# Graph attention on one core: the aggregation of the four heads in halves of 256 columns

## The reference

```python
h = (x @ W).reshape(N, H, C)
al_s = jnp.einsum('nhc,hc->nh', h, a_src)
al_d = jnp.einsum('nhc,hc->nh', h, a_dst)
e = jax.nn.leaky_relu(al_s[src] + al_d[dst], NEG_SLOPE)
m = jax.ops.segment_max(e, dst, num_segments=N)
ex = jnp.exp(e - m[dst])
denom = jax.ops.segment_sum(ex, dst, num_segments=N)
alpha = ex / (denom[dst] + 1e-16)
msg = h[src] * alpha[:, :, None]
out = jax.ops.segment_sum(msg, dst, num_segments=N)
...
h = jax.nn.elu(_gat_layer(x, src, dst, W1, att_src1, att_dst1, b1, concat=True))
out = _gat_layer(h, src, dst, W2, att_src2, att_dst2, b2, concat=False)
...
x = _layernorm(x + out)
```

## Time and profile before

| | |
|---|---|
| Time, median of 3 runs | 1033.69 us (1031.19 to 1034.45) |
| The profiled execution | 1031.99 us, of which its span (first to last instruction) is 1030.2 us |
| PE busy | 913.7 us, 89% of the span, 4740 instructions |
| Weight loads | 786.4 us, 76% |
| DVE / ACT / POOL busy | 619.3 / 401.3 / 210.1 us |
| The four heads (aggregation and `make`) | from 220 to 676 us of the span |

### The profile page before, as it was taken

How to read it: one execution, slowest core, us unless ns; L and a number is a source line. 1 busy time by engine, 2 the same in 40 slices (tenths; PEclk the granted TensorE clock), 3 DMA queues, 4 the chain that set the end, 5 groups by cost and what they waited for, 6 DMA issues and landing times.

```text
span 1030.2 us, 13905 instructions
## 1 busy us (share of the span) xinstructions
PE 913.7 (89%) x4740; PEld 786.4 (76%) x4740; DVE 619.3 (60%) x1305; ACT 401.3 (39%) x574; POOL 210.1 (20%) x113
## 2 busy tenths in 40 slices
PE   0676788979999999999999999979999998479996
PEld 0454566668787788878887788869999998479995
DVE  9666568379987456863578645443221222988874
ACT  6454531256651366514663155542111112622220
POOL 1002000225530145202442023410000000343432
PEclk9987999989999999999999999989999999689998
DMA  6009975040115410263003431252111100101122
GB/s 155 1 7 191 150 227 171 7 128 27 32 32 191 179 31 29 66 219 126 30 30 102 138 103 37 93 191 111 58 63 40 74 6 1 44 21 57 59 64 69
DMA packets 38710, 86.65 MB, mean 84 GB/s; under 512 B 17251, under 2 KB 17411, under 8 KB 37032
## 3 DMA queue, kind: packets, MB, share of 16 engines
q1 hardware_dynamic: 38663, 86.04, 29.1%
HBM read 64.27 MB, written 21.76 MB: 84 GB/s over the span
## 4 chain that ended last, share of the span: by engine, by line
issue 38%; PE 27%; DVE 10%; ACT 8%; POOL 8%; SPq 4%; DMA 4%; DVEq 0%; POOLq 0%; ACTq 0%
PE ps L1243 7%; PE ps L1245 7%; PE ps L1244 7%; POOL prow L419 5%; SPq L501 4%; DVE junk_w L1032 2%; POOL W1lo L629 2%; PE ps L1353 2%; DMA hidden_scratch<-ebuf 2%; DMA xT_scratch<-xa 1%; PE ps L1274 1%; ACT prow L414 1%; DVE nbr L437 1%; DVE prow L456 1%; ACT oh_lo L701 1%
## 5 line engine op out<-in xcount | busy, mean ns | idle before, releaser
L419 POOL TENSOR_TENSOR prow<-prow,arow 125x1250 f32<-125x1250 f32 x50 | 139.3, 2789 | 633.4 <-ACT prow L414 633.4
L1243 PE MATMUL ps<-hhi,PThi 125*125 125x512 f32 x400 | 162.2, 405 | 1.0 <-DVE hlo L1019 1.0
L1244 PE MATMUL ps<-hlo,PThi 125*125 125x512 f32 x400 | 158.5, 396 | 0.0
L1245 PE MATMUL ps<-hhi,PTlo 125*125 125x512 f32 x400 | 158.1, 395 | 0.0
L425 ACT ACTIVATE prow<-prow,expb 125x1250 f32<-125x1250 f32 x50 | 67.0, 1340 | 172.7 <-POOL prow L419 151.5
L1243 PE MATMUL ps<-W2p,hT 128*125 128x384 f32 x320 | 110.6, 346 | 6.7 <-DVE W2p L1129 5.6
L1245 PE MATMUL ps<-W2p,hT 128*125 128x384 f32 x320 | 108.7, 340 | 0.0
L1244 PE MATMUL ps<-W2p,hT 128*125 128x384 f32 x320 | 108.5, 339 | 0.0
L1088 DVE TENSOR_TENSOR hT<-ps,hT 128x500 fp32r<-128x500 f32 x40 | 25.3, 674 | 128.4 <-ACT hT L797 124.0
L476 PE MATMUL ps<-ident,prow 125*125 125x125 f32 x500 | 68.1, 286 | 28.4 <-DVE prow L456 12.2
L476 PEld LDWEIGHTS ps<-ident,prow 125*125 125x125 f32 x500 | 65.0, 199 | 35.0 <-issue 30.6
(11 more groups left out here) (157 smaller groups left out, 1818.2 us busy)
## 6 DMA issues: line engine op xcount, KB each, us to landing
xr<-xT_scratch SPq DMA_DIRECT2D x30, 750.0 KB, 4.4
hidden_scratch<-ebuf SPq DMA_DIRECT2D x40, 250.0 KB
hblk<-hidden_scratch SPq DMA_DIRECT2D x10, 1000.0 KB
xT_scratch<-xa SPq DMA_DIRECT2D x20, 375.0 KB, 13.2
w1raw<-in_L_gnn_W SPq DMA_DIRECT2D x4, 1536.0 KB, 7.7
w1raw<-in_L_gnn_W SPq DMA_DIRECT2D x12, 512.0 KB, 3.6
w2late<-in_L_gnn_W SPq DMA_DIRECT2D x10, 384.0 KB, 8.0
xres<-in_x SPq DMA_DIRECT2D x10, 375.0 KB
```

The source lines that it names most:

```text
L419: pool.tensor_tensor(buf[:, s, :], buf[:, s, :], row, ALU.add).then_inc(e_done, 1)
L1243: pe.matmul(dst, ahi, bhi, start=start, stop=False)
L1244: pe.matmul(dst, ahi, blo, start=False, stop=False)
L1245: return pe.matmul(dst, alo, bhi, start=False, stop=stop)
```

## The change

In the aggregation of the four heads, each source block's three products over 512 columns are replaced by two times three products over 256 columns: first all three for the columns 0 to 255, then all three for 256 to 511, in the same PSUM bank. Only the first product of the whole bank has `start`, as before. `products` gets an argument that hands `skip_group_check` on to the builder; it changes no instruction. Nothing else is edited: `make`, both products of the second layer, and all the work of the other engines stay.

```diff
-            def products(dst, parts, start, stop):
+            def products(dst, parts, start, stop, shared=False):
                 (ahi, alo), (bhi, blo) = parts
-                pe.matmul(dst, ahi, bhi, start=start, stop=False)
-                pe.matmul(dst, ahi, blo, start=False, stop=False)
-                return pe.matmul(dst, alo, bhi, start=False, stop=stop)
+                pe.matmul(dst, ahi, bhi, start=start, stop=False, skip_group_check=shared)
+                pe.matmul(dst, ahi, blo, start=False, stop=False, skip_group_check=shared)
+                return pe.matmul(dst, alo, bhi, start=False, stop=stop, skip_group_check=shared)
...
                     for b in range(NB):
-                        t = products(PS[0:B, s, :], ((PThi[:, s, b, :], PTlo[:, s, b, :]), (hhi[:, b, :], hlo[:, b, :])),
-                                     b == 0, b == NB - 1)
+                        for c in (0, HC // 2):
+                            t = products(PS[0:B, s, c:c + HC // 2],
+                                         ((PThi[:, s, b, :], PTlo[:, s, b, :]),
+                                          (hhi[:, b, c:c + HC // 2], hlo[:, b, c:c + HC // 2])),
+                                         b == 0 and c == 0, b == NB - 1, True)
                     t.then_inc(mm_done, 1)
```

## The result

The changed kernel takes 1037.38 us (median of 12 runs, 1034.85 to 1039.23), the one before 1033.53 us (median of 12). The ratio is 1.004, with a 95% interval of 1.0026 to 1.0054: 2.7 to 5.6 us slower. One of the 12 runs of the kernel before took 1083.38 us, in a slower state, and is left out of the ratio.

What follows compares the result with a forecast made beforehand. It took PE to bound the aggregation: 1200 products becoming 2400 add 3.8 us, less 0.3 us absorbed, so +3.5 us on the median of 1033.7 gives 1037.2 us. The range was 1032 to 1046 us.

Steps and rivals of the forecast that it cites:

- TensorE bounds the heads: In the heads' aggregation PE is always busy, so a product's gain or loss reaches the end almost one for one.
- T: Price of one 256-column product in the aggregation, forecast at 117.8 ns against 232.5 for 512 columns; +3.8 us in all.
- line B: Price per column from rows with 8 stationary columns, 500 and 250 streaming: 0.451 ns per column, +1.3 ns a pair, +1.6 us.
- line A: Price per column from rows with 125 stationary columns, 384 and 512 streaming: 0.446 ns per column, +4.1 ns a pair, +4.9 us.
- The cover holds: Each weight load, 110.5 ns, stays hidden beside the product ahead of it in the aggregation, with 7 ns to spare.
- The first rival: Load cover gone or excess paid per product in the aggregation: 19.2 ns each, +23.0 us, 1056.7 us; chance 0.17 with its lesser variant.
- smaller form: Load and stream so close in the aggregation that jitter holds either up: 121 ns per product, +11.4 us, 1045; within the 0.17.
- The third rival: Faster: 256 columns start as often as 250, at 114.1 ns, in the aggregation; -5.2 us, 1028.5 us; chance 0.07.
- The sequencer: PE's sequencer issues two instructions per product in 70 ns, so it stays ahead in the aggregation; no cost.
- the second rival: PE's sequencer falls behind in the aggregation, at 124 ns per product: +18.6 us, 1052 us; chance 0.05.
- What is absorbed: Added time hidden in head 0's waits for DVE and ahead of the W2 product: 0.3 us off in all.
- The fourth rival: No measurable effect: added time absorbed ahead of the W2 product, or a half costs just half of 232.5 ns; 1033.7 us, chance 0.05.

Runs made afterwards that it cites:

- e10: Kernel before, with products in the first two steps of head 3 cut into 384+128 columns, all else in 512: 1037.84 us, ratio 1.0029.
- e6: Kernel before, with halves of 256 columns in heads 1, 2 and 3 and head 0 left in 512: 1037.74 us, ratio 1.004.
- e3: Changed kernel with 64 stationary columns instead of 125 in nine of ten source blocks, halves in heads 0 and 1, 512 columns in heads 2 and 3: 1036.17 us.
- e1: Changed kernel with the cut elsewhere in each head: 384+128, 320+192, 288+224, 272+240 in heads 0 to 3: 1056.56 us, ratio 1.0219.
- e7: The kernel before, unchanged, run and profiled once more: 1036.22 us in its one run.
- e8: The changed kernel, with nothing further edited, run and profiled once more: 1040.20 us in its one run.
- e5: Kernel before, with halves of 256 columns in head 0 alone and the other heads in 512: 1034.54 us, ratio 1.0008.
- e4: Changed kernel with 128 stationary columns instead of 125 in nine of ten source blocks, halves in heads 0 and 1, 512 in heads 2 and 3: 1039.85 us.
- e2: Changed kernel with the two halves of each product next to each other, so the same operand is loaded twice in a row: 1037.24 us, ratio 1.0033.

## Why the prediction was right, point by point

- **TensorE bounds the heads, so a product's price passes.** Right for the heads 1 to 3 up to the loads of the hidden blocks: e10 passed all of its 3.2 us, and e6 has 2.4 of the whole change's 2.8 to 3.1 us in the stretch of the heads.
- **T.** I took 117.8 ns, two thirds of the way from line B to line A. It is 118.4, line A to a tenth. The term was to be +3.8 us and is +5.3. The step that was off is the blend: line A has the edited product's own width of stationary operand and would have been right alone, and I moved a third of the way to line B. Why line B is low is not shown. Its row of 250 columns is 1.6 ns below line A (114.1 against 118.4 less 6 x 0.446), its row of 500 only 0.2 (226.9 against 227.1), while e3, with 64 columns loaded and 64 rows written, gained 1.5 and 2 ns at 256 and 512. A price that simply grows with the load's width does not give both.
- **The cover holds.** Right, and e1 shows where it ends: at 224 columns and fewer the load sets the pace, at 109 to 110 ns. The first rival, in its fixed form (19.2 ns per product, +23.0 us), is out: the excess at 512 columns goes with the columns. In its smaller form (T = 121 ns) it did not come. I gave it 0.17; in e3 the halves gained no more from a shorter load than the long products did, so nothing of the thin cover is felt at 256. The third rival, T below 114.9 ns, did not come either.
- **The sequencer.** Right, and with it the second rival, 124 ns per product, is out: PE's sequencer now passes the wait and the ten transposes from 507.0 to 507.7, in the same 0.7 us as before, and the transposes start at 508.64. The branches of PE's loops take at most 230 ns, 237 before. The two rows of the changed kernel:

```profile
L1362 PEldq ALU_OP  x1: 36/36/36, 507.0 to 507.0; - x1
```

```profile
L1369 PEldq ALU_OP  x1: 32/32/32, 507.7 to 507.7; - x1
```

- **What is absorbed.** The term that was mis-sized most: "I take 0.3 us off in all". It is about 2.2 (5.3 less the 3.1 of the first pair of profiles). 0.7 go in eight steps of head 0, which I had put at a few tenths from a single wait of 0.24 us. Two of its steps are longer than the others by 0.4 and 0.6 us (8.49 and 8.63, e7), of which the wait on the page shows only a part; the length of such a step over its neighbours is what I should have read. 0.1 goes in head 0's first step, whose end is a wait for DVE in both kernels: from its first product to the next transposes it takes 9.11 us before (220.18 to 229.29) and 9.12 after (223.75 to 232.87). 0.9 go at the end of the heads, where I had counted 0.3: I took the three steps behind the issue, but the issue itself hangs on a product some 6 us further up, and whatever is added behind that product is hidden too. Another 0.4 go in the waits for DMA in `make`, 2.1 us before and 1.7 after, with the same 1.7 in e6 and e8; I had not counted them. The wait in the kernel before, and in the changed one (us in total, times, longest):

```profile
PE ps L1243 <- DMA xr<-xT_scratch: 2.1, 3, 1.0
```

```profile
PE ps L1243 <- DMA xr<-xT_scratch: 1.7, 3, 0.6
```

  These four make 2.1; the rest is within what the profiles repeat to.
- **The sum.** +3.8 - 0.3 = +3.5 was forecast; +5.3 - 2.2 = +3.1 is what the profiles show between the heads and W2, and +3.9 is the difference of the medians, with an interval of 2.7 to 5.6. Two errors of 1.5 and 1.9 us had opposite signs. The total is close to the forecast in part by luck: with only one of them it would have come to +5.0 or +1.6 us.
- **Slower rather than the same.** The interval of the ratio begins at 1.0026, so the time is likelier beyond my bound of 0.3% than within. The fourth rival, absorbed altogether, holds for head 0 alone (e5) and not for the change.

The small difference between odd and even steps (119.0 and 117.9 ns; 232 and 233 in the kernel before) goes with the buffer, `s` 0 or 1. In e4, where the loads are 128 columns wide, it is gone at 256 columns: the 58 starts take 6.86 to 6.88 us in both kinds of step of head 1. So it hangs on the load of 125 columns and the buffer together; why is open.

## What to carry to other kernels

In this kernel a dense row of products costs the distance between starts, columns times a slope plus a few ns per product, and never less than the weight load beside it. Splitting a product in two costs that per-product part once more as long as both parts stay above the load (here 4.4 ns a pair), and much more beyond: read the price from rows with the same stationary width, since rows with another one were off by 1 to 2 ns here, as much as the part sought. Before multiplying by the count, look for places where the engine already waits for others: an added microsecond passed in full in one step of this kernel and vanished in another of the same loop. And where executions of one kernel differ by as much as the effect, compare stretches of the traces that begin with the same product.

## What the runs showed of the hardware that I had not expected

- The width of the stationary operand shows in the price even when its load is wholly beside a product twice its length: 64 instead of 125 columns, with 64 rows written instead of 125, take 2 ns off a product of 512 columns (e3). It is no straight line: 128 columns cost the same as 125 (e4), and 8 columns with 500 streaming cost 226.9 ns, where line A has 227.1 for 125.
- A float32r product of 512 columns takes 232.5 ns at the clock of 2.4 GHz, where half of the 426.7 ns at 1.2 GHz (granted clock 0.50 from 220.7 to 223.4 us) would be 213.3. The excess of 19.2 ns grows with the columns (9.9 ns at 250). The narrower operand of e3 takes 2 of the 19 away, and the order of the products nothing (e2); the cause of the rest stays open.
- The uneven cut costs by the pair and not by the part: in head 0 of e1 the starts of six products, 384 three times and 128 three times, follow each other irregularly, and only their sum of 0.85 us per source block is steady. Rows of e1, one source block:

```profile
259.55 0.22 PE L1243 MATMUL ps<-hhi,PThi 125*125 125x128 f32 x1
259.60 0.28 PE L1244 MATMUL ps<-hlo,PThi 125*125 125x128 f32 x1
259.71 0.27 PE L1245 MATMUL ps<-hhi,PTlo 125*125 125x128 f32 x1
259.82 0.39 PE L1243 MATMUL ps<-hhi,PThi 125*125 125x384 f32 x1
260.05 0.33 PE L1244 MATMUL ps<-hlo,PThi 125*125 125x384 f32 x1
260.22 0.34 PE L1245 MATMUL ps<-hhi,PTlo 125*125 125x384 f32 x1
260.40 0.22 PE L1243 MATMUL ps<-hhi,PThi 125*125 125x128 f32 x1
```

The first product of 128 columns is followed after 0.05 us, presumably since its successor's load was already done behind the long product; the two after it pay the load's 0.11. The first of 384 takes 0.23, the two after it 0.17 and 0.18.
